# Four blocks in one launch: the last attention's scores in two sets of banks, biases weighed early, a new order of the set-up and of the middle groups

## The reference

```python
# L0 mixer: causal convolution along the tokens with a complex decaying filter per channel
y = (conv(filt, x) + last_conv * phazor_progression * phazor).real * gate
# L0 FFN: 8 experts of width 64 (top 2 of a softmax) and a shared one of width 128
out = sum_e coef_e * (silu(x@gate_e) * (x@up_e)) @ down_e + shared(x)
# L1 attention: 16 heads of 64, l2-normed q and k, two null keys, ALiBi bias, causal
xn  = layernorm(x) * gamma;  q, k = l2norm(...), l2norm(...)
out = softmax(8*q@k.T - slope*|distance|) @ v @ w_out
# L1 FFN: 4 different experts, top 2; e0 SwiGLU, e1 GELU MLP, e2 two layernorms and relu, e3 GELU MLP
out = (rw[..., None] * gathered(stack([e0, e1, e2, e3]))).sum(2)
```

## Time and profile before

| | us |
|---|---|
| median of 3 runs | 929.02 (928.15 to 929.4) |
| the profiled execution's own time | 928.41 |
| its span, first to last instruction | 926.60 |
| busy: PE / DVE / ACT / POOL | 860.1 / 779.7 / 586.2 / 587.7 |
| stage: set-up and first group up to the attention | 0 to 64.4 |
| FIRST, attention of group 0 | 64.4 to 156.2 |
| MIDDLE, five groups | 156.2 to 688.8 |
| LAST_L | 688.8 to 792.4 |
| LAST_A | 792.4 to 888.9 |
| LAST_F | to 926.6 |

### The profile page before, as it was taken

How to read it: one execution, slowest core, us unless ns; L and a number is a source line. 1 busy time by engine, 2 the same in 40 slices (tenths; PEclk the granted TensorE clock), 3 DMA queues, 4 the chain that set the end, 5 groups by cost and what they waited for, 6 DMA issues and landing times.

```text
span 926.6 us, 25509 instructions
## 1 busy us (share of the span) xinstructions
PE 860.1 (93%) x10110; PEld 700.6 (76%) x10110; DVE 779.7 (84%) x2457; ACT 586.2 (63%) x1255; POOL 587.7 (63%) x632
## 2 busy tenths in 40 slices
PE   0998899999999999999999999999999999999886
PEld 0675688787877878788787878678787888777676
DVE  6788799889998899989988899889998688955587
ACT  4428683966568672966648673876728684686631
POOL 5118774688637973678735974478735865569623
PEclk9999899999999999999999999999999999999999
DMA  5400000000000000000000000000000000000000
GB/s 161 118 1 1 12 3 2 1 13 2 15 1 1 13 2 14 1 13 2 4 12 1 13 3 15 0 13 2 3 13 1 1 3 14 1 1 2 15 1 12
DMA packets 22008, 11.73 MB, mean 13 GB/s; under 512 B 7552, under 2 KB 21248, under 8 KB 21760
## 3 DMA queue, kind: packets, MB, share of 16 engines
q1 hardware_dynamic: 20032, 9.50, 3.7%
q10 hardware_dynamic: 1856, 0.59, 0.3%
HBM read 7.99 MB, written 2.10 MB: 11 GB/s over the span
## 4 chain that ended last, share of the span: by engine, by line
PE 49%; DVE 38%; ACT 7%; issue 4%; POOL 2%; DMA 0%; DVEq 0%; ACTq 0%; POOLq 0%
PE bank L1771 8%; PE bank L1772 7%; PE bank L1773 7%; PE bank L1784 5%; DVE x4m L1723 3%; PE bank L2036 3%; DVE qT L1623 2%; DVE mixed L1620 2%; PE bank L2042 2%; PE bank L1999 2%; PE bank L2204 1%; DVE bank L1609 1%; DVE xn L1399 1%; PE bank L2211 1%; DVE conv L1451 1%
## 5 line engine op out<-in xcount | busy, mean ns | idle before, releaser
L937 POOL TENSOR_TENSOR rnorm<-sumsq,minus_half 128x16 f32<-128x16 f32 x32 | 95.4, 2990 | 55.6 <-DVE sumsq L1574 55.3
L943 POOL TENSOR_TENSOR rnorm<-unit,minus_half 128x16 f32<-128x16 f32 x32 | 93.1, 2916 | 3.1 <-DVE unit L1580 3.1
L1202 ACT ACTIVATE square<-bank,bias_k,rnorm 128x256 f32<-128x256 f32 x128 | 65.7, 570 | 44.8 <-PE bank L2036 44.8
L2042 PE MATMUL bank<-qT,kT 64*64 64x64 f32 (+1 forms) x1024 | 82.9, 253 | 5.6 <-ACT unit L1208 3.3
L2036 PE MATMUL bank<-qT,kT 64*64 64x256 f32 (+1 forms) x1024 | 84.4, 358 | 0.0
L952 POOL TENSOR_SCALAR_AFFINE_SELECT square<-square 128x256 f32<-128x256 f32 x128 | 61.8, 509 | 34.3 <-ACT square L1208 34.3
L1132 ACT ACTIVATE xaT_hi<-bank 128x256 fp32r<-128x256 f32 x16 | 6.0, 384 | 115.3 <-PE bank L1951 114.7
L952 POOL TENSOR_SCALAR_AFFINE_SELECT unit<-unit 128x256 f32<-128x256 f32 x128 | 48.5, 407 | 37.9 <-ACT unit L1208 37.9
L2042 PEld LDWEIGHTS bank<-qT,kT 64*64 64x64 f32 x1024 | 51.9, 132 | 20.8 <-ACT unit L1208 6.9
L2118 PE MATMUL bank<-w_out,qT 128*128 128x128 f32 x512 | 62.8, 276 | 1.5 <-DVE qT L1623 1.5
L1202 ACT ACTIVATE unit<-bank,bias_k,rnorm 128x256 f32<-128x256 f32 x96 | 51.5, 575 | 17.7 <-PE bank L2036 16.3
(11 more groups left out here) (423 smaller groups left out, 2996.2 us busy)
## 6 DMA issues: line engine op xcount, KB each, us to landing
xin<-in_L_attn_x SPq DMA_DIRECT2D x7, 256.0 KB, 2.8
out<-x SPq DMA_DIRECT2D x7, 256.0 KB, 2.3
square<-in_L_attn_w_kv SPq DMA_DIRECT2D x1, 1024.0 KB, 6.5
unit<-in_L_attn_w_q SPq DMA_DIRECT2D x1, 512.0 KB, 5.8
w_out<-in_L_attn_w_out SPq DMA_DIRECT2D x8, 64.0 KB, 2.1
xin<-in_L_attn_x ACTq DMA_DIRECT2D x1, 256.0 KB, 3.1
unit<-in_L_ffn_experts_gate ACTq DMA_DIRECT2D x1, 256.0 KB, 3.3
unit<-in_L_ffn_experts_up SPq DMA_DIRECT2D x1, 256.0 KB, 2.8
```

The lines of the kernel that those rows point to most:

```text
L937: pool.tensor_tensor(rnorm[:, 1, t, :], sumsq[:, t % 2, :], minus_half[:], ALU.pow).then_inc(a_root.sem, 1)
L943: pool.tensor_tensor(rnorm[:, 0, ts, hs], k_sumsq[:, ts, hs], minus_half[:, hs].unsqueeze(1).to_broadcast([P, 2, H // 2]), ALU.pow).then_i ...
L1202: last = act.activation(early(pr, j), k0, ACT.Exp, bias=bias_k0[:, h:h + 1], scale=by)
L2042: return mm(bank[2][cs, 2 * P * s + P * i:2 * P * s + P * i + n], kT[rs, p, tile1 + 64 * k:tile1 + 64 * k + 64], qT[rs, p, tile1:tile1 + n ...
```

## The change

1. **Last attention.** In the group that ends, `score_banks` gives units 2, 4 and 6 the banks 4 to 6 and the others banks 0 to 2. PE's `a_scores(c)` then waits for the exponentials of unit c-2 (unit 2: for the weighing of `f_out.2`), ACT's exponentials of unit c wait for the values of unit c-2 (`a_pv`), and the values use bank 3 alone, so each waits for DVE's division of the one before (`a_mix`). Unit 2 writes its banks whole instead of leaving out the masked corners. POOL's sum of the late parts gets a home in `conv`. In LAST_A's list of PE `a_scores.0` and `a_nT` go ahead of `f_out.0`, `a_scores.1` behind `f_out.1`, `a_scores.2` ahead of `a_mix.0`: from there scores are two units ahead of values.
2. **Biases early.** For group 6 POOL's `f_bias` writes to `conv` and no longer waits for the turned rows (`f_gT`). In LAST_A it moves from behind `a_kss.0.1` to behind `a_ss.2`, DVE's and ACT's `f_pick` and POOL's `a_keep` move ahead, and so does `a_nexp`. The last expert's hidden rows lie in other tiles (`ml_last`) for group 6, without a wait for `a_ss`.
3. **Set-up.** Of six `s_warm` two stay. `s_kv` on ACT scales and rounds `w_kv` in four halves between other steps; its low part goes to POOL (`s_kvlo`, two halves). `s_w0` is played in two parts, `s_qlo` and `s_raw` behind `l_turn3`, `s_nk` behind `l_xl.1`. PE's `s_turn` goes ahead of `l_turn3`, its null-key transpose is a step of its own (`s_nkz`), `s_fold4` is played in three parts. POOL clears its tiles ahead of `l_res`, and its root of the null keys and `s_colb` wait until the first group's layernorm is applied (`n_l.steps`). In `e_sum` the wait for the last filter stands behind the first addition.
4. **Middle lists.** MIDDLE's four lists are other ones. On DVE `f_pick` goes from behind `a_u.1` to behind `l_res`, `a_nexp` ahead of `l_turn3`, `f_out.0` ahead of `l_route`, `e_apply`, `l_cT`, `l_hc` and `e_sum` some places back, `f_end` ahead of `a_mix.6`; on PE `f_out.0` goes ahead of `l_turn3`, `l_g.0` ahead of `f_out.2`, `a_nT` behind `f_out.3`; on POOL one half of `a_kss.0` goes ahead of `f_ce2`.

```diff
 PROLOGUE "PE"
-e_turn1 l_turn2 s_warm.0 s_warm.1 s_warm.2 s_warm.3 l_turn3 s_turn l_route l_g.0 s_fold1 l_u.0 l_g.1 s_warm.4 l_u.1
+e_turn1 l_turn2 s_warm.0 s_warm.1 s_turn l_turn3 l_route l_g.0 s_fold1 s_nkz l_u.0 l_g.1 s_fold4.0 l_u.1
...
-l_g.2 ... s_fold3 l_u.4 l_c.3 s_warm.5 l_down.0 l_down.1 l_down.2 l_down.3 s_fold4 l_x.0 l_x.1
+l_g.2 ... s_fold3 l_u.4 l_c.3 s_fold4.1 l_down.0 l_down.1 l_down.2 l_down.3 s_fold4.2 l_x.0 l_x.1
 PROLOGUE "DVE"
-... e_sum l_turn2 s_w0 l_res s_scale l_norm s_raw l_turn3 l_route ... l_hu.4 s_v2 s_kvlo s_qlo l_dstats.0 ... s_nk l_xl.0 s_split l_xl.1
+... e_sum s_w0.0 l_turn2 s_w0.1 l_res s_scale l_norm l_turn3 s_raw s_qlo l_route ... l_hu.3 s_v2 ... l_hu.4 l_dstats.0 ... l_xl.0 s_split l_xl.1 s_nk
 MIDDLE "PE"
-l_turn3 f_out.0 l_route f_out.1 a_scores.0 a_nT f_out.2 l_g.0 f_out.3 a_scores.1 l_u.0 l_g.1 l_cT a_mix.0 a_scores.2 a_mix.1 e_turn1 l_u.1
+f_out.0 l_turn3 f_out.1 l_route a_scores.0 l_g.0 f_out.2 f_out.3 a_nT a_scores.1 l_u.0 l_g.1 a_mix.0 a_scores.2 a_mix.1 l_u.1 e_turn1
 MIDDLE "DVE"
-l_res l_norm l_turn3 e_stats a_nexp l_route l_pick l_coef f_out.0 a_nT f_out.1 l_hg.0 f_out.2 f_out.3 f_end_stats e_apply a_mix.0
+l_res f_pick l_norm a_nexp l_turn3 e_stats f_out.0 l_route l_pick f_out.1 l_hg.0 l_coef f_out.2 f_out.3 f_end_stats a_nT a_mix.0
 LAST_A "PE"
-a_v.3 f_out.0 f_out.1 a_scores.0 f_out.2 f_out.3 a_scores.1 a_nT a_mix.0 a_scores.2 a_mix.1 a_scores.3 ... a_scores.7 a_out.0 a_mix.6 a_mix.7
+a_v.3 a_scores.0 a_nT f_out.0 f_out.1 a_scores.1 f_out.2 f_out.3 a_scores.2 a_mix.0 a_scores.3 a_mix.1 ... a_scores.7 a_mix.5 a_out.0 a_mix.6 a_mix.7
 LAST_A "POOL"
-... a_ss.1 f_ce f_ce_apply a_ss.2 a_ss.3 f_ce2 a_kss.0.0 a_kss.0.1 f_bias a_kss.1.0 a_kss.1.1 a_scores.0 a_scores.1 a_keep f_end_stats
+... a_ss.1 f_ce a_keep f_ce_apply a_ss.2 f_bias a_ss.3 f_ce2 a_kss.0.0 a_kss.0.1 a_kss.1.0 a_kss.1.1 a_scores.0 a_scores.1 f_end_stats
...
+        def score_banks(g, c):
+            return bank[4:7] if ending(g) and c and c % 2 == 0 else bank[0:3]
...
+            def s_kvlo(h):
+                cols = slice(h * H * DH, (h + 1) * H * DH)
+                pool.wait_ge(qkv_rounded, 2 + h)
+                pool.tensor_tensor(w_kv.lo[:, cols], w_kv_raw[:, cols], w_kv.hi[:, cols].bitcast(F32), ALU.subtract).then_inc(kv_split, 1)
...
 ACT score_exps
+                if ending(g) and c > 1:
+                    act.wait_ge(a_pv.sem, a_pv.at(g, c - 1))
...
 PE a_scores
-                else:
-                    pe.wait_ge(a_exp.sem, a_exp.at(g, 4 * c))
+                elif not ending(g) or c == 1:
+                    pe.wait_ge(a_exp.sem, a_exp.at(g, 4 * c))
+                elif c == 2:
+                    pe.wait_ge(f_eb.sem, f_eb.at(g - 1, 3 * E1))
+                else:
+                    pe.wait_ge(a_exp.sem, a_exp.at(g, 4 * c - 4))
```

More of the change, by code:

```diff
@@ L86 @@
     "PE": """
[L87 to L91, removed]
@@ L92 @@
-l_down.1 l_down.2 a_mix.7 l_down.3 a_out.0 a_out.1 l_x.0 l_x.1
+a_m.0 a_m.1 a_null a_k.0 f_turn.0 f_turn.1 f_ce.0 f_ce.1 a_k.1 f_sw.0 f_me.0 a_kr.0 a_t.0 a_m.2 f_ceT f_sw.1 a_k.2
+a_k.3 f_relu.0 f_sw.2 a_t.1 a_m.3 a_kr.1 f_relu.1 f_sw.3 a_kt f_ce2 a_v.0 l_turn2 f_ml.0 f_ml.1 a_t.2 a_v.1 f_me.1
+f_ce2T a_t.3 a_v.2 f_ml.2 f_ml.3 a_v.3 f_out.0 l_turn3 f_out.1 l_route a_scores.0 l_g.0 f_out.2 f_out.3 a_nT
+a_scores.1 l_u.0 l_g.1 a_mix.0 a_scores.2 a_mix.1 l_u.1 e_turn1 l_g.2 a_scores.3 a_mix.2 l_u.2 l_cT a_scores.4
@@ L93 @@
+a_mix.3 l_g.3 l_u.3 l_c.0 a_scores.5 l_g.4 a_mix.4 l_c.1 a_scores.6 l_c.2 a_mix.5 l_u.4 l_c.3 a_scores.7 a_mix.6
+l_down.0 l_down.1 l_down.2 a_mix.7 l_down.3 a_out.0 a_out.1 l_x.0 l_x.1
 """,
     "DVE": """
-f_stats.0 f_stats.1 f_apply.0 f_apply.1 a_ss.0 f_turn.0 a_null f_turn.1 f_ce f_route a_u.0 f_ce_apply f_hid.0 a_ss.1
-a_ss.2 f_hid.1 a_u.1 f_pick a_u.2 f_hid.2 a_ss.3 a_kss f_hid.3 f_ce2 l_turn2 a_u.3 f_ce2_apply l_res l_norm l_turn3
-e_stats a_nexp l_route l_pick l_coef f_out.0 a_nT f_out.1 l_hg.0 f_out.2 f_out.3 f_end_stats e_apply a_mix.0 l_hu.0
@@ L98 @@
-l_hg.1 a_mix.1 l_cT l_hu.1 e_scan a_mix.2 l_hg.2 l_hu.2 a_mix.3 l_hc.0 l_hg.3 l_hc.1 e_sum l_hu.3 a_mix.4 l_hc.2
-a_mix.5 l_hg.4 l_hu.4 l_hc.3 a_mix.6 f_end l_dstats.0 a_mix.7 l_end.0 l_dstats.1 l_astats.0 l_end.1 a_o.0 l_astats.1
-a_end.0 l_aapply.0 l_aapply.1 a_o.1 l_xl.0 l_xl.1 a_end.1
+f_stats.0 f_stats.1 f_apply.0 a_null f_apply.1 a_ss.0 f_turn.0 f_turn.1 f_ce f_route a_u.0 f_ce_apply f_hid.0 a_ss.1
+a_ss.2 f_hid.1 a_u.1 a_u.2 f_hid.2 a_ss.3 a_kss f_hid.3 f_ce2 l_turn2 a_u.3 f_ce2_apply l_res f_pick l_norm a_nexp
@@ L101 @@
+l_turn3 e_stats f_out.0 l_route l_pick f_out.1 l_hg.0 l_coef f_out.2 f_out.3 f_end_stats a_nT a_mix.0 l_hg.1 e_apply
+l_hu.0 a_mix.1 l_hu.1 e_scan a_mix.2 l_cT l_hg.2 l_hu.2 a_mix.3 l_hg.3 l_hc.0 l_hu.3 a_mix.4 l_hc.1 l_hg.4 e_sum
+l_hc.2 a_mix.5 l_hc.3 l_hu.4 f_end a_mix.6 l_dstats.0 a_mix.7 l_dstats.1 l_end.0 l_end.1 l_astats.0 a_o.0 l_astats.1
+l_aapply.0 a_end.0 l_aapply.1 a_o.1 l_xl.0 l_xl.1 a_end.1
 """,
     "ACT": """
-a_m.0 a_m.1 f_turn.0 f_turn.1 a_k.0 a_k.1 f_me.0 f_sw.0 a_t.0 f_pick f_ceT a_m.2 f_sw.1 a_k.2 f_relu.0 a_k.3 a_t.1
@@ L2083, in a_mix_ @@
                     pe.wait_ge(l_conv.sem, l_conv.at(g + 2, 2))
-                if ending(g) and c > 1:
-                    pe.wait_ge(a_mix.sem, a_mix.at(g, 4 * c - 4))
-                elif c and not ending(g):
-                    pe.wait_ge(a_mix.sem, a_mix.at(g, 4 * c))
                 den = bank[7][:, 0:2 * P]
-                parts = [pv_bank(g, c)[:, 2 * P * f:2 * P * (f + 1)] for f in range(2)]
+                parts = [bank[3][:, 2 * P * f:2 * P * (f + 1)] for f in range(2)]
                 for rs, h, pr, j in quad:
```

218 lines of the change are left out of this document (121 added, 97 removed).

## The result

The changed kernel takes 918.57 us (median of 4 runs, 917.87 to 919.4) against 928.81 (928.15 to 929.4): ratio 0.989, 95% interval 0.9873 to 0.9907. The forecast was 919.0. The sum came out within 0.5 us, but none of its three terms did, so the stages come first. A stage begins where DVE takes the low part of the attention's input.

What follows compares the result with a forecast made beforehand. In a middle group PE's list sets the pace first, DVE's from about 305.5 on. Set-up -3.9, middle lists -1.5 and last attention -4.6 sum to -10.0, 919.0 us against the median of 929.02; range 914.5 to 923, chance 0.50.

Steps and rivals of the forecast that it cites:

- Set-up: Chain through the first group's layernorms and FFN: -3.9 us in all, ends -5.5 and -1.5.
- `l_norm`'s apply: Set-up: four tiles in 1.12 instead of 2.54, as POOL's clearing and column copies lie elsewhere: -1.4 us.
- `l_turn2`'s apply: Set-up: it waits only for the root, at about 24.1, no longer behind the low part of `w_up`: -1.3 us.
- POOL's low part of `w_kv`: Set-up: two halves of some 2.5 us under the routing may hold up small DVE steps: +0.4, between 0 and +2.5.
- Middle groups: Middle lists, five times: -0.3 us per group, ends -1.2 and +1.0, together -1.5.
- the early `f_out.0`: Middle seam, PE: put ahead of `l_turn3`, it makes the turned rows and DVE's low part come later: +2.4 us.
- `a_nexp`, the wait for the weighings and the hold-up: Middle groups, DVE: `a_nexp` leaves the full stretch -1.5, `f_out.0` waits for POOL's weighings +0.4, one hold-up by POOL less -0.95.
- the exchanges among projections and FFN: Middle groups, stretch set by PE: half of the 1.12 wait, -0.6 us, between 0 and -1.4.
- rival D: Middle lists cost 0.5 to 1.5 us per group, B's mechanism half hidden: 923 to 927; chance 0.08.
- rival A: Middle seam: both DVE waits filled, nothing paid back, 2.5 us per group, 12.5 instead of 1.5: 908; chance 0.20.
- Last attention: Earlier biases and norms, ACT no longer waiting for scores, units of 3.45 to 3.7: -4.6 us, ends -3.5 and -6.
- rival E: Last attention: exponentials wait for values of unit c-2, period near 4.4, only 1.5 us gained: 922; chance 0.06.

Runs made afterwards that it cites:

- `kv_late`: The changed kernel, with POOL's first half of the low part of `w_kv` also waiting for the weights that `l_coef` ends with: 919.09 us.
- `mid_front`: The kernel before with the changed middle lists up to `l_route`, `l_pick`, `l_exp` and the last of `a_kss`, old orders behind: 933.68 us, ratio 1.0053.
- `mid_only`: The kernel before with the changed middle lists alone: 923.39 us, ratio 0.9944.
- `mid_old`: The changed kernel with the four middle lists of before: 924.69 us.
- `best_a`: The changed kernel with the late `w_kv` half, `f_out.0` behind `l_turn3` in MIDDLE and `a_nT` behind `f_out.0` in LAST_A: 917.18 us, ratio 0.9874.
- `fout_back`: The changed kernel with `f_out.0` behind `l_turn3` again on PE's middle list: 919.03 us.
- `best_b`: `best_a` with one idle batch of five matmuls on PE ahead of `l_x.0`: 917.75 us, output wrong, only its time counts.

## Why the prediction was right, and where it was not

The direction was right. That the total came so close was luck: the set-up gave 3.5 us less than forecast and the middle groups 3.4 more, and the last attention's 1.3 less was mostly made up by 0.9 in stages that were put at nothing. Set-up and last attention lie outside their own ends (-1.5 and -3.5); the middle groups lie inside theirs, for another reason than the one given.

- **Set-up, -3.9 predicted, -0.44 in the trace.** `l_norm`'s apply came as said (1.12). Two terms were too large: `l_turn2`'s apply began only 0.39 earlier, not 1.9, as DVE's first addition took 1.01 beside POOL's last filter and POOL's root 1.53; and `s_turn` ran until 31.41 where the rows of `l_turn3` were ready at 30.88. These two are the miss up to the router's sum, -1.06 against the -3.1 of the working; no run tries them. The failed step behind it is POOL's low part of `w_kv`, taken at +0.4 inside ends of 0 and 2.5: it cost 2.2 on the one small step with both operands in SBUF, and PE waited 1.61 behind it. `kv_late` shows that, and gets 1.9 of set-up back. The rule that I set beside it, SBUF — State Buffer, Who interferes with whom, of the Trainium skill, is borne out by the step itself: a DVE step with two inputs in SBUF and a POOL instruction that reads SBUF keep each other out for a whole instruction, 2.35 beside 2.38, and 0.69 is unchanged with an operand in PSUM.
- **Middle groups, -0.3 each predicted, -0.98 measured.** The terms of the seam were right: the early `f_out.0` makes the turned rows 2.5 later (2.4 in the working), and `a_nexp`, the wait for the weighings and the hold-up give 2.1 back behind them (-1.5+0.4-0.95, that is -2.05). The -0.6 for the exchanges among projections and FFN did not come; that stretch is 0.4 longer. So the changed front alone loses 0.75 per group at full clock, 1.0 by the median of `mid_front`, which is rival D. What I left out was the second half. I costed the places of `l_cT`, `e_apply`, `a_nT` and `f_end` at nothing, without looking at what PE and POOL did beside them; `mid_front` against `mid_only` puts 1.6 us per group there at full clock, 2.0 by the medians. Neither the forecast nor rival A (which put its gain into the seam) has this mechanism.
- **One group of the five.** 0.8 of the 4.92 is the fourth group of before, 107.13 against 106.33 to 106.41, in which the granted clock was 0.98; `mid_old` shows it too (107.04) and `mid_front` in its fifth (108.61), the traces with the changed lists don't. Why there, stays open.
- **Last attention, -4.6 predicted, -3.33 measured.** The bank sets did what was said, units of 3.7 us (846.44 to 864.91 for five of them). The exponentials of unit 7 ended 3.7 earlier in the stage than before, where the working has 4.3: unit 2 began 0.7 later than put there, as its wait for the values of unit 0 was 5.80, and units 4 and 6 waited 0.8 each for values (rival E in small). From there to the last `a_out` it took 6.7, where the working has 6.0 and before it was 6.3: PE waited 0.70 for the single value bank, and 0.88 for the last division (1.45 before).
- **FIRST and LAST_L**, -0.55 and -0.39, were not predicted. FIRST lies within what single executions differ by (91.6 to 93.6 over these fourteen traces). LAST_L's 0.4 is in `mid_old` and not in `mid_only`, so it comes with the rest of the change; which part was not tried.

## What to carry to other kernels

A list written by hand is changed as a whole: the first half of this one, alone, was a loss of 5 us and the second made it a gain of 5. Cutting each group where one engine hands over to another, and reading both parts, showed where each half paid. Before a large elementwise step is moved to POOL, list the DVE steps beside it whose operands all lie in SBUF: each may take as long as POOL's instruction, however small it is. A second set of buffers needs its scores early, and what is pushed back for that (most of 2.7 here) is to be set against its gain (6.0 here).

## What the runs showed of the hardware

- A DVE product of 128x8 took 2.35 us beside POOL's 2.38 and 0.16 without; four applies of SBUF rows took 2.51 beside POOL's mask of 0.77 and addition of 1.27, and 1.26 with only a mask of 0.76 beside their end.
- Executions of one kernel differ by 1 to 5 us, and the mean granted clock alone does not order them: 917.38 at 0.992 and 919.1 to 919.3 at 0.988 for `kv_late`, but 916.39 at 0.987 and 917.1 at 0.992 for `best_a`, and 917.67 and 920.26 both at 0.990 for `fout_back`. The five middle groups of one trace with the changed lists agree within 0.1.
- The clock can fall with PE busy: in `best_b` it was 0.72 on average from 56 to 60 (1.00 until 57, 0.50 from 58), while PE ran `s_fold4.2` without a wait.
